# First attention layer: score levels stored as distance below the row maximum, made by pairs of heads, with the small operations on GpSimd

## The reference, cut to what matters

```python
q, k, v = (to_heads(q), to_heads(k), to_heads(v))      # 16 batches, 16 heads, 224 rows, 64
dots = jnp.einsum('bhnd,bhmd->bhnm', q, k) * temp
dots = fq_floor(dots)
attn = jax.nn.softmax(dots, axis=-1)
attn = fq_floor(attn)
out = jnp.einsum('bhnm,bhmd->bhnd', attn, v)
```

## Time and profile before

| | us |
|---|---|
| median of 3 runs (lowest, highest) | 4358.63 (4355.87, 4361.25) |
| profiled execution, span from first to last instruction | 4348.3 |
| TensorE busy in the span | 3429.6 (79%) |
| VectorE busy | 2546.7 (59%) |
| ScalarE busy | 1685.4 (39%) |
| GpSimd busy | 795.3 (18%) |

### The profile page before, as it was taken

One profiled execution on the slowest core, in us unless ns is written; L12 is line 12 of the kernel. 1 busy time (PEld: TensorE's weight loads), 2 busy tenths in 40 slices (PEclk: granted clock), 3 DMA queues, 4 the chain that ended last, 5 costly groups with the idle time before them and its releaser, 6 DMA issues. The chain is left out here.

```text
span 4348.3 us, 76007 instructions
## 1 busy us (share of the span) xinstructions
PE 3429.6 (79%) x30617; PEld 2482.9 (57%) x30658; DVE 2546.7 (59%) x3800; ACT 1685.4 (39%) x3064; POOL 795.3 (18%) x454
## 2 busy tenths in 40 slices
PE   0887731139584899999999999977995199999994
PEld 0343321126334777777777777744553199999993
DVE  8679878879983555555455555536875133333333
ACT  2222279978412333333333433322221133333332
POOL 0000000000000333333433334330000511111110
PEclk9999865555596999999999999978997599999997
DMA  3400032223123001110001110003200433333325
GB/s 150 179 1 1 30 102 80 79 78 95 45 99 124 20 29 33 48 32 29 28 28 33 35 45 28 10 5 87 48 21 20 168 98 101 82 92 86 82 43 149
DMA packets 140159, 276.40 MB, mean 64 GB/s; under 512 B 43464, under 2 KB 43464, under 8 KB 135776
## 3 DMA queue, kind: packets, MB, share of 16 engines
q1 hardware_dynamic: 124208, 239.60, 17.5%
q0 software_dynamic: 14592, 30.44, 4.0%
q10 hardware_dynamic: 1072, 2.10, 0.2%
HBM read 158.02 MB, written 102.23 MB: 60 GB/s over the span
## 5 line engine op out<-in xcount | busy, mean ns | idle before, releaser
L1608 DVE TENSOR_REDUCE arena<-psum 112x4 f32<-112x1504 f32 x256 | 440.1, 1719 | 303.0 <-PE psum L1429 302.6
L1573 ACT ACTIVATE arena<-psum 125x1792 f32<-125x1792 f32 x192 | 320.2, 1668 | 289.4 <-PE psum L1443 289.4
L1337 POOL TENSOR_TENSOR arena<-arena 125x896 f32<-125x896 f32 x128 | 269.7, 2107 | 681.6 <-ACT arena L1573 681.6
L1342 POOL TENSOR_TENSOR arena<-arena 125x896 f32<-125x896 f32 x128 | 269.3, 2104 | 292.6 <-ACT arena L1573 287.6
L802 ACT ACTIVATE arena<-arena,scales 112x224 bf16<-112x224 int8 x512 | 286.0, 559 | 35.6 <-DVEq L787 35.5
L717 PE MATMUL psum<-arena 64*112 64x224 bf16 x512 | 63.6, 401 | 274.6 <-DVEq L786 261.7
L2518 DVE TENSOR_TENSOR gelu_T_rest<-arena,gelu_T_high 128x384 fp32r<-128x384 f32 (+1 forms) x192 | 104.5, 547 | 269.2 <-ACT gelu_T_high L2464 269.2
L2379 PE MATMUL psum<-tokens_T_high,w_high 128*128 128x384 f32 (+1 forms) x768 | 255.5, 333 | 1.6 <-DVE tokens_T_rest L2493 1.6
L2381 PE MATMUL psum<-tokens_T_high,w_rest 128*128 128x384 f32 (+1 forms) x768 | 254.8, 332 | 0.0
L2380 PE MATMUL psum<-tokens_T_rest,w_high 128*128 128x384 f32 (+1 forms) x768 | 254.6, 332 | 0.0
L2357 POOL DMA_INDIRECT x_plus_h_rows<-arena x72 | 114.6, 1592 | 731.6 <-DVE arena L2528 727.3
(11 more groups left out here) (362 smaller groups left out, 8738.8 us busy)
## 6 DMA issues: line engine op xcount, KB each, us to landing
arena<-L_ffn_moe_w SPq DMA_DIRECT2D x16, 2048.0 KB, 11.0
arena<-ctx SPq DMA_DIRECT2D x16, 1500.0 KB
rows_by_slot<-arena SPq DMA_DIRECT2D x1, 18200.0 KB, 52.1
arena<-x SPq DMA_DIRECT2D x14, 1024.0 KB, 13.4
arena<-arena SPq DMA_DIRECT2D x16, 896.0 KB, 7.0
arena<-x_after_attn SPq DMA_DIRECT2D x32, 448.0 KB, 16.3
dots_ints<-arena SPq DMA_DIRECT2D x16, 784.0 KB, 4.8
arena<-dots_ints SPq DMA_DIRECT2D x16, 784.0 KB, 5.6
```

The source lines that it names most:

```text
L1337: G.tensor_tensor(some_exps[:, r, :, :], prob[:, t, :, 0:NS], prob[:, t, :, NS:2 * NS], ALU.add).then_inc(paired, 1)
L1342: G.tensor_tensor(some_exps[:, 0, :, :], some_exps[:, 0, :, :], prob[:, 1, :, s * NS:(s + 1) * NS], ALU.add).then_inc(paired, 1)
L1573: S.activation(prob[:, t, :, :], score_psum(MC, 2 * NS), ACT.Exp, scale=SCALE2).then_inc(exp_done, 1)
L1608: return V.tensor_reduce(rmx[:, i // 2, i % 2, :], score_psum(HALF, HC), axis=AX.X, op=ALU.max).then_inc(r_free, 1)
```

## The change

The levels are kept as uint8 and are the distance itself, from 0 up; the offset LOW and the column `lowest` are gone, and both exponentials (lines 802 and 910) are written without a bias. The stage works on pairs of heads instead of groups of four: NP = 8 pairs a batch, 128 in all, each 112 x 896 scores, in DB = 4 sets of two PSUM banks. VectorE takes the largest of pair n+1 before it writes the distances of pair n. The two small operations on the row maxima are issued on GpSimd, as straight code of 128 repetitions. `bank_free` is gone: TensorE waits for `lv_ready` of four pairs back. VectorE waits for `exp_done` of sixteen pairs back instead of two groups. VectorE's own stream has the first two batches as straight code and the others in a loop of 7 turns (`loop1`, moved up from the stage behind).

```diff
-I8 = mybir.dt.int8
+U8 = mybir.dt.uint8
...
-LOW = 128.0
...
-                ch.link(V.tensor_scalar(col("below"), col("c_d"), -0.5, 0.5 - LOW, ALU.mult, ALU.add))
-                ch.link(V.tensor_scalar(col("lowest"), col("s_d"), -LOW, None, ALU.mult))
+                ch.link(V.tensor_scalar(col("below"), col("c_d"), -0.5, 0.5, ALU.mult, ALU.add))
...
+        NP = H1 // 2
+        DB = 4
...
+        def pair_psum(pr):
+            return psum[0:HALF, 2 * (pr % DB):2 * (pr % DB) + 2, 0:2 * NS]
...
+                            for pr in range(NP):
+                                pe.wait_ge(lv_ready, (i + u) * NP + pr + 1)
+                                for j in range(2):
+                                    at = slice(DH1 * j, DH1 * (j + 1))
+                                    for half in range(2):
+                                        last = PE.matmul(psum[0:HALF, 2 * (pr % DB) + j, half * NS:(half + 1) * NS],
+                                                         stage[at, u, pr, half * HALF:(half + 1) * HALF],
+                                                         stage[at, u, IN1 // P + pr, :], start=True, stop=True)
+                                last.then_inc(mm_done, 1)
...
                 @block.vector
                 def _(dve):
-                    dve.sem_inc(bank_free, 2)
...
-                                ch = Chain(dve, chs, n * 4)
-                                dve.wait_ge(mm_done, n + 1)
-                                dve.wait_ge(exp_done, n + 1)
-                                raw = group_psum(hg).rearrange("p h (a n) -> p h a n", a=2)
-                                ch.link(V.tensor_reduce(rmf[:, g, :], raw, axis=AX.X, op=ALU.max))
-                                ch.link(V.tensor_scalar(rm16[:, g, :], rmf[:, g, :], col("off_d")[0:HALF], col("c_d")[0:HALF],
-                                                        ALU.add, ALU.mult))
-                                ch.link(V.tensor_scalar(top_g[:, g, :], rm16[:, g, :], col("below")[0:HALF], None, ALU.add))
-                                ch.link(V.scalar_tensor_tensor(
...
+                    def largest(b, pr):
+                        n = b * NP + pr
+                        dve.wait_ge(mm_done, n + 1)
+                        V.tensor_reduce(rmf[:, pr % 2, :], pair_psum(pr).rearrange("p h (a n) -> p h a n", a=2), axis=AX.X, op=ALU.max).then_inc(max_found, 1)
+
+                    def below_largest(b, u, pr):
+                        n = b * NP + pr
+                        if pr == 0:
+                            dve.wait_ge(stored[u], stored_count(b, u))
+                        dve.wait_ge(exp_done, n + 1)
+                        dve.wait_ge(top_ready, n + 1)
+                        V.scalar_tensor_tensor(
+                            d8[:, u, 2 * pr:2 * pr + 2, :].rearrange("p h (a n) -> p h a n", a=2),
+                            pair_psum(pr).rearrange("p h (a n) -> p h a n", a=2), col("minus_c_d")[0:HALF],
+                            top_g[:, pr % 2, :].rearrange("p (h a) -> p h a", a=2).unsqueeze(3).broadcast_to([HALF, 2, 2, NS]),
+                            ALU.mult, ALU.add).then_inc(lv_ready, 1)
+
+                    def body(b, u, first):
+                        for pr in range(NP):
+                            largest(b, pr)
+                            if pr >= 1:
+                                below_largest(b, u, pr - 1)
+                            elif not first:
+                                below_largest(b - 1, 1 - u, NP - 1)
+                    dve.sem_inc(lv_ready, DB)
+                    loop1(dve, body)
+                    below_largest(NB - 1, 1, NP - 1)
+
+                @block.gpsimd
+                def _(pool):
+                    for n in range(NB * NP):
+                        pool.wait_ge(max_found, n + 1)
+                        G.tensor_scalar(rm16[:, n % 2, :], rmf[:, n % 2, :], col("off_d")[0:HALF], col("c_d")[0:HALF],
+                                        ALU.add, ALU.mult).then_inc(max_levelled, 1)
+                        pool.wait_ge(max_levelled, n + 1)
+                        if n >= 2:
+                            pool.wait_ge(lv_ready, n - 1 + DB)
+                        G.tensor_scalar(top_g[:, n % 2, :], rm16[:, n % 2, :], col("below")[0:HALF], 1.0, ALU.add, ALU.mult).then_inc(top_ready, 1)
...
-                                act.wait_ge(lv_ready, n + 1)
...
-                                for j in range(2 * HG):
-                                    h = hg * HG + j // 2
-                                    last = S.activation(junk[:, hg % 2, j, :], d8[:, u, h, (j % 2) * NS:(j % 2 + 1) * NS], ACT.Exp,
-                                                        bias=col("lowest")[0:HALF], scale=col("minus_s_d")[0:HALF],
+                                act.wait_ge(lv_ready, n + 1 + DB)
...
+                                for j in range(4):
+                                    h = 2 * pr + j // 2
+                                    last = S.activation(junk[:, pr % 2, j, :], d8[:, u, h, (j % 2) * NS:(j % 2 + 1) * NS], ACT.Exp,
+                                                        scale=col("minus_s_d")[0:HALF],
...
-                        sp.wait_ge(lv_ready, b * NG + NG)
+                        sp.wait_ge(lv_ready, b * NP + (NP + DB))
...
-                            S.activation(e[:, pr % 2, :, :], d8[:, u, 2 * pr:2 * pr + 2, :], ACT.Exp, bias=col("lowest")[0:HALF],
+                            S.activation(e[:, pr % 2, :, :], d8[:, u, 2 * pr:2 * pr + 2, :], ACT.Exp,
                                          scale=col("minus_s_d")[0:HALF]).then_inc(exp_done, 1)
```

More of the change, by code:

```diff
@@ L19 @@
 SBUF = 200 * 1024
-SIZE = {F32: 4, I32: 4, U32: 4, BF16: 2, I16: 2, I8: 1}
+SIZE = {F32: 4, I32: 4, U32: 4, BF16: 2, I16: 2, U8: 1}
 P = 128
@@ L147, in decoder_kernel @@
         v_d = scratch("v_ints", (NB * 2, HALF, IN1), BF16)
-        d_d = scratch("dots_ints", (NB, HALF, H1 * NS * 2), I8)
+        d_d = scratch("dots_ints", (NB, HALF, H1 * NS * 2), U8)
         x1_d = scratch("x_after_attn", (T, D))
@@ L703, in decoder_kernel, with loop1 @@
         L1a.close()
-        HG = 4
-        NG = H1 // HG
+        NP = H1 // 2
+        DB = 4
         def stage_count(i, u):
             return i * 8 + 16
[L711 to L723, removed]
+        def pair_psum(pr):
+            return psum[0:HALF, 2 * (pr % DB):2 * (pr % DB) + 2, 0:2 * NS]
+        def loop1(eng, body):
+            body(0, 0, True)
+            body(1, 1, False)
+            with eng.Fori(0, NB // 2 - 1) as pair:
+                for u in range(2):
+                    body(pair * 2 + (u + 2), u, False)
         rsum = sb("row_sum", [HALF, NB, 2 * H1], F32, L1)
@@ L732, in _, with stored_count @@
                 ch.link(V.tensor_scalar(col("minus_c_d"), col("c_d"), -1.0, None, ALU.mult))
-                ch.link(V.tensor_scalar(col("below"), col("c_d"), -0.5, 0.5 - LOW, ALU.mult, ALU.add))
-                ch.link(V.tensor_scalar(col("lowest"), col("s_d"), -LOW, None, ALU.mult))
+                ch.link(V.tensor_scalar(col("below"), col("c_d"), -0.5, 0.5, ALU.mult, ALU.add))
         with ExitStack() as st:
[L738 to L741, removed]
+            d8 = sb("levels_below_row_max", [HALF, 2, H1, 2 * NS], U8, st)
+            rm16 = sb("row_max_levels", [HALF, 2, 4], I16, st)
+            rmf = sb("row_max_raw", [HALF, 2, 4], F32, st)
+            top_g = sb("row_max_of_pair", [HALF, 2, 4], F32, st)
             rs_g = sb("row_sum_of_batch", [HALF, 2, 2 * H1], F32, st)
-            junk = sb("exp_unused", [HALF, 2, 2 * HG, NS], BF16, st)
-            with phase("dq", "g0", "g1", "us", "mm", "fr", "ch", "lv", "ac", "ex", "rs", "s0", "s1") as (block, (
-                    staged0, staged1, used, mm_done, bank_free, chs, lv_ready, group_read, exp_done, sum_kept, st0, st1)):
+            junk = sb("exp_unused", [HALF, 2, 4, NS], BF16, st)
+            with phase("dq", "g0", "g1", "us", "mm", "rr", "rl", "tp", "lv", "ex", "rs", "s0", "s1") as (block, (
+                    staged0, staged1, used, mm_done, max_found, max_levelled, top_ready, lv_ready, exp_done, sum_kept, st0, st1)):
                 stored = (st0, st1)
                 staged = (staged0, staged1)
+                def stored_count(b, u):
+                    return b * 8 + (16 if u == 0 else 8)
                 @block.tensor
@@ L756, in _ @@
                             pe.wait_ge(staged[u], stage_count(i, u))
[L757 to L760, removed]
+                            for pr in range(NP):
[7 more added lines that the diff above has]
+                                last.then_inc(mm_done, 1)
+                            pe.wait_ge(mm_done, (i + u) * NP + NP)
                             pe.sem_inc(used, 1)
@@ L789, in _ @@
                 @block.scalar
                 def _(act):
-                    act.sem_inc(exp_done, 2)
+                    act.sem_inc(exp_done, 2 * NP)
                     with act.Fori(0, NB // 2) as pair:
```

(23 more changed lines are left out.)

## The result

The changed kernel takes 4295.8 us (median of four launches), the kernel before 4358.44 in the same comparison; the ratio is 0.9856 with a 95% interval of [0.9843, 0.987]. In a second comparison with five launches of it, it was 4294.42 against 4359.13, 0.985 [0.9837, 0.9864]. One of the four launches of the first comparison took 9848 us and is left out of the ratio; the median of the other three is 4295.0. The prediction said 4292, range 4284 to 4322.

A forecast was written before the change was run, and what follows sets the result against it. VectorE's chain of 5.14 us per group of four heads was taken to bound the score stage. Savings of 65.3 us there, 1 in the next stage and 0.2 in the preparation gave 4358.6 - 66.5 = 4292, range 4284 to 4322.

The forecast's parts named there:

- VectorE's pair: Score stage: reduction 1.08 plus subtraction 1.15 less two overlaps of 0.08 is 2.07 us a pair, 265 us for 128 pairs.
- the cheaper exponential: Score stage, ScalarE: without a bias from SBUF an exponential falls from 0.559 to about 0.466 us, 48 us off ScalarE.
- the covered latency: Score stage: GpSimd's 0.8 us from a reduction's end to the subtraction's release stays hidden, as does anything under 2.07 us.
- Rival A: Score stage: neighbouring VectorE instructions do not overlap, a pair costs 2.23 us, 20.5 us more, 4313; chance 0.14.
- The 3.5 us for seven turns: Score stage, VectorE: each of the loop's seven turns adds 0.5 us, the difference of 0.90 and 0.41, 3.5 in all.
- rival B: Score stage: the missing bias is still given as a pointer, so ScalarE is the bound, 35.4 us later, 4328; chance 0.07.
- Rival C: Score stage: GpSimd's latency decides, paid by half from 2.07 us; gain gone at 1.4 us an operation; chance 0.06.
- The stage: Score stage: ends with the last store at 856.9 instead of with the copy at 922.24, 65.3 us less.
- the 6 us of the Trainium skill: GpSimd's first call of freshly loaded code: about 5 us worse if behind the first reduction, nothing if under the first transfer.
- The next stage: Stage behind the score stage: 12 us of cheaper exponentials, but VectorE sets it; 1 us taken, bounds 0 and 8.7.
- the preparation: Preparation: one tiny operation less, 0.2 us saved.
- 10.3 us: Kernel before: difference between the profiled span of 4348.3 and the runs' median of 4358.63, said to lie around the span.

## Why the prediction was right

The mechanism was right in its main steps inside the stage: VectorE's pair, the cheaper exponential, the covered latency. That the time came out only 3.8 us above the forecast (2.4 in the second comparison) is partly luck: two misses of 5 to 6 us cancelled.

- **VectorE's pair.** 2.07 forecast, 2.056 measured. The reduction was taken from a row of the same size and is 1.077; the subtraction, from a line through two other sizes, was 1.15 and is 1.137. Rival A, no overlap between neighbours, is refuted: starts lie 0.08 closer than durations, for the subtraction too. By the rule of the Trainium skill, "VectorE: DVE Perf Modes", "The DRAIN you can't avoid", a pair would have been 2.21; the trace does not agree. The same section adds that a next operation that is not held starts earlier, which the prediction left out; that sentence agrees with the overlap of 0.08.
- **The loop.** The 3.5 us for seven turns were not there: VectorE went from 589.32 to 852.86, 263.5 us, and 128 x 2.056 is 263.2. I take it that the queue now runs ahead of the engine, where the old chain held it by a signal; no experiment separates that.
- **ScalarE.** Each exponential 0.467 (0.466 forecast), the missing bias is not a pointer even beside a scale from SBUF: rival B is out, and the experiment with the bias back gives its time, 4336 against the 4328 worked out for it (that estimate lacked the 5.8 us below). ScalarE stayed just under VectorE, 256.7 and 263.7 us busy. It began later than reckoned, 4.8 us after the first reduction and not 3.2, since a table load of 1.28 us now stood behind the first levels; that cost nothing, as the last store ended the stage.
- **GpSimd in the stage.** 0.25 us was assumed for an operation; they are 0.345 and 0.263, with 0.1 for each hand-over 0.91 in all where 0.8 was forecast, far inside the cover of 2.06. Rival C did not come about, and its formula was wrong where it was tested, at 2.7 us of latency: five and one operations in a row gave a period of 2.45 by GpSimd's throughput. By an estimate from that, the break-even would have lain at a period of 2.56 and about 1.2 us an operation, not at the 1.4 of rival C.
- **The stage.** 582.62 to 856.9 was forecast, 274.3 us; it was 588.65 to 857.73, the first operation of the next stage, 269.1. The some 5 us that it is better are 3.5 for the loop and 1.8 for the pair.
- **The step that failed: nothing was charged behind the stage for GpSimd.** The reduction over partitions follows the small operations on the same engine and now takes 5.8 us longer to answer (6.32 against 0.48 before and with the small operations on VectorE, and 0.49 when another is issued early). The prediction had quoted the 6 us of the Trainium skill ("GPSIMD Engine Reference", section 2.1, "Instruction dispatch") for the first call of freshly loaded code, but looked for it only at the first small operation, where nothing of it shows: that one began 0.32 us after its reduction, against 0.1 later in the stage. The 5.86 us of the early issue agree with the figure; the place was missed. That it is the loading of code is the page's explanation; what the runs show is the delay, that it needs the small operations on GpSimd ahead of it, and that one early reduction takes it.
- **The next stage.** 1 us was forecast, VectorE's idle time for ScalarE there fell by 1.0:

```profile
L948 DVE TENSOR_SCALAR arena<-arena 112x224 bf16<-112x224 f32 x512 | 136.3, 329 | 10.9 <-ACT arena L920 7.7 <-DVE arena L940 3.2
L920 ACT ACTIVATE arena<-arena,scales 112x896 f32<-112x896 uint8 x128 | 133.4, 1044 | 24.0 <-DMA arena<-v_ints 22.7 <-issue 1.0 <-DVE arena L948 0.3
```

The sum with the measured terms: 339.9 to 269.1 in the stage is -70.8, the reduction over partitions +5.8, the next stage -1.0, the preparation -0.2: -66.2. The runs say -62.6 and -64.7. The remaining 1.5 to 3.6 us are within what single executions of either kernel differ by, up to 11 us, and stay unassigned.

What was wrong in the reasoning although the time does not show it: 10.3 us were said to lie around the span. It is 1.9; the profile of before was a quick execution. The two profiled spans differ by 55.2 us, 11 less than the forecast 66.5: judged by them alone the forecast would have looked far worse than by the medians.

## What to carry to other kernels

Read every operand that a diff drops: an exponential of 224 columns lost 0.09 of its 0.56 us with its bias from SBUF, and where two engines are close to each other as the bound, relieving both pays far more than the sum of each (1 and 23 us alone, 65 together). To take a small dependent step off a busy engine, hand it to an idle one and put a neighbour's work in between; the same move without that order was 1.4% slower than before. Count what the helper engine has to do next: GpSimd's change from small operations to a reduction over partitions cost 6 us behind the stage, and one early call hid it.

## What the runs showed of the hardware that was not expected

- GpSimd with small operations of four columns on 112 partitions, chained by semaphores, repeats one each 0.44 us (0.343 for the operation), and 0.91 us pass between the end of a VectorE reduction and the start of the VectorE instruction that waits for two such operations.
- The first reduction over partitions after them begins 5.8 us later than otherwise, both when it had waited for its input (5.91 us after that was written) and when it had nothing to wait for (5.86 us after the last small operation); the next one does not.
- A stretch that no edit touched (queries and keys) ran at a mean granted clock of 0.89 or 0.86 in different executions, of either kernel, and took about 6 us more at the lower. So a comparison of the spans of two single profiles can contain it.
